# Two key buffers at the start, and four 16-node additions per round behind a transpose, in a graph layer on one core

## The chip, the cores and the metric

The kernel runs on one core of a Trainium2 chip. The metric is the device time of one execution in microseconds (us). Before the change it is 2062.51 us, the median of three runs (2060.89 to 2064.04).

## The reference

A graph layer over 12,500 nodes of 128 features and 400,000 edges, sorted by destination:

```python
Xs = X[src]
m_data = Xs @ W_data.T + b_data
m_ctrl = Xs @ W_control.T + b_control
msg = jnp.where((edge_types == 0)[:, None], m_data, m_ctrl)
agg = jax.ops.segment_sum(msg, dst, num_segments=X.shape[0])
out = jax.nn.relu(agg + (X @ W_self.T + b_self))
y = layernorm(x + out)          # over the 128 features, eps 1e-5
```

## The kernel before

The kernel never forms messages. It sums source rows by destination and edge type first, and multiplies the two sums of a node by the two weight matrices afterwards. Nodes are split into two sets.

**Dense nodes** (the first 6400). Their sums are products of x with a matrix of edge counts. TensorE builds the counts of 20 nodes (a batch) out of one-hot matrices that VectorE makes (`make_onehots`, L1176 to L1190). ScalarE, and for the last half batch of eight VectorE (`move_last`, L1195 to L1204), copies them out of PSUM, and TensorE multiplies them with x (`apply`, L738). There are 640 batches, one in each **step** s of the main loop, eight to a pass. In step s TensorE does `apply(s-8)`, then `build(s)` (L719), then whatever small job that step has. At the start of a pass `apply` waits for `move_last`. The one-hots need keys of the edges. Fifteen chunks of keys are prepared on VectorE (`prepare_dense_keys`, L1079 to L1090), chunk 1 in step 1 and chunks 2 to 14 in steps 9 to 21, and stored to memory by SyncE's queue (`store_dkeys`, L499 to L505). All chunks share one buffer, `dk_f`, which lies over `x_u`, so chunk c waits until the store of chunk c-1 has landed. Later the keys are gathered back in groups of 240 nodes. To find a group's place, a window of 129 destinations is loaded (`load_window`, L482), and `find_starts` (L1118 to L1129) reads it. `win_i` is a single buffer.

**Sparse nodes** (the rest) go through 154 **rounds**. In a round GpSimd gathers ten times 128 rows of x (L637, two rounds ahead at most), TensorE multiplies them with one-hots (`gather_sums`, L699), in step s-1. ScalarE copies the result to `sg`: 128 partitions, each one place of a (half, sub-window, type, node) list, by 128 features. In step s TensorE turns it into `misc` (`turn_sums`, L746 and L747), and VectorE adds it to the accumulator `acc` at a place read from memory (`add_sums`, L1234 to L1249). Each of a round's two groups covers two windows of 16 nodes that overlap (the second begins 9 nodes on). The matrix `turn_picks` of ones and zeros adds the overlap in the matmul, so `misc` holds 32 nodes of two types per group.

Every small job of TensorE writes the one bank `misc`: rounds, key groups, and for each of 114 output units a transpose of x (`turn_x`, L763) and the products (L778 to L789). Before each job TensorE waits on `misc_free` for the reader of the job before it. For a round that is VectorE's increment at L1249, after both groups are added. Rounds sit in steps 4 and 0 of a pass of eight; the planner at the top of the kernel puts every other job into the next free step. TensorE works strictly in the written order, as do the others.

Of the kernel before, what the change touches and what calls it, by code (L numbers as in the profile page):

```python
# [13 lines left out]
ALU = mybir.AluOpType  # L14
# [3 lines left out]
P = 128  # L18
D = 128
GT = 5  # L20
WIN = 32
HALF_WIN = 16
LATE_WIN = 9
# [30 lines left out]
DKCH = 15  # L54
# [5 lines left out]
def gnn_resnorm(nc, x, src, dst, etype, w_data, b_data, w_ctrl, b_ctrl, w_self, b_self, out):  # L60
# [6 lines left out]
    KGROUPS = -(-DENSE // KNODES)  # L67
# [48 lines left out]
    for e in range(EPOCHS):  # L116
        base = WIN_0 + EPOCH_NODES * e
        n0 = max(base, DENSE)
        n1 = N if e == EPOCHS - 1 else base + EPOCH_NODES
        k = -(-(n1 - n0) // P)  # L120
# [23 lines left out]
    for v in units:  # L144
        if not v.dense:
            e = (v.n0 - WIN_0) // EPOCH_NODES
# [59 lines left out]
    with ctx:  # L206
        def sb(name, shape, dt=F32):
            return ctx.enter_context(nc.sbuf_tensor(name, shape, dt))
# [5 lines left out]
        def sem(name):  # L214
            return ctx.enter_context(nc.semaphore(name))
# [16 lines left out]
        acc = sb("acc", [P, 2, 2, SPAN])  # L232
# [7 lines left out]
        ident = sb("ident", [P, P])  # L240
# [5 lines left out]
        part_f = sb("part_f", [P, 10])  # L246
# [3 lines left out]
        low = sb("low", [P, 2])  # L250
        base_p = sb("base_p", [P, 3, 2])
        sg = sb("sg", [P, 129])
        turn_picks = sb("turn_picks", [P, P])
        fin = sb("fin", [P, 2, COLS])
        fin_deg = sb("fin_deg", [P, DEG_RING * KNODES], BF16)
        deg_c = sb("deg_c", [P, 2, 9], BF16)
# [1 line left out]
        deg_new = sb("deg_new", [P, 2])  # L258
        deg_ok = sb("deg_ok", [P, 2])
        x_u = sb("x_u", [P, 3, D])  # L260
        x_t = sb("x_t", [P, 2, P])
        y_sb = sb("y_sb", [P, 2, D])
        stats = sb("stats", [P, 2, 6])
        mv = sb("mv", [P, 2, 2])
        std = sb("std", [P, 2])
# [6 lines left out]
        ptr = sb("ptr", [P, 4, 2])  # L272
# [34 lines left out]
        iota_q, iota_p = iotas[:, 0:2 * XBLOCKS], iotas[:, 2 * XBLOCKS:2 * XBLOCKS + P]  # L307
# [20 lines left out]
        K = KCOLS  # L328
# [1 line left out]
        acc_1 = acc_1f.bitcast(I32)  # L330
        dk_in = [[acc_1[:, K * (3 * i + k):K * (3 * i + k + 1)] for k in range(3)] for i in range(2)]
        dk_p = acc_1[:, 6 * K:7 * K]
        dk_f = x_u[:, :, :].rearrange("p u d -> p (u d)")[:, 0:3 * K]
        b9_f = acc_1f[0:9, 7 * K:7 * K + D]
        b9_h = acc_1f[0:9, 7 * K + D:7 * K + D + D // 2].bitcast(BF16)
        assert 7 * K + D + D // 2 <= 2 * SPAN and 3 * K <= 3 * D

        acc_all = cnt_raw[:, 0:XBLOCKS * P]
        late_x = x_u[:, 0, :]
        late_xt = x_t[:, 0, :]  # L340
        LW = 256
        iota_w = acc[:, 0, 0, 0:LW]
# [12 lines left out]
        misc = psum("misc")  # L355
# [32 lines left out]
        weights_turned = sem("weights_turned")  # L388
        wt_ready = sem("wt_ready")
        dkeys_ready = sem("dkeys_ready")  # L390
        dkeys_written = sem("dkeys_written")
        tail_ready = sem("tail_ready")
        hi_ready = sem("hi_ready")
        x2_ready = sem("x2_ready")
        win_taken = sem("win_taken")
# [9 lines left out]
        acc_step = sem("acc_step")  # L405
# [6 lines left out]
        misc_full = sem("misc_full")  # L412
# [40 lines left out]
        key_flat = key_dram.rearrange("r w -> (r w)").rearrange("(c p e) -> c p e", c=DKCH, p=P)  # L453
        key0_flat = key0_dram.rearrange("r w -> (r w)").rearrange("(p e) -> p e", p=P)
        key1_flat = key1_dram.rearrange("r w -> (r w)").rearrange("(c p e) -> c p e", c=2, p=P)
# [8 lines left out]
            return KEY_TILES * P if g >= 3 else K * P * min(2, g + 1)  # L464

        def key_stores(c):
            return 16 * (c + 1 + min(c + 1, 2) + 1)

        KEY_STORES = key_stores(DKCH - 1)

        def late_rows(u):
            return min(P, N - u * P)
# [3 lines left out]
        def _(sp):  # L476
# [22 lines left out]
            def store_dkeys(c):  # L499
                sp.wait_ge(dkeys_ready, c + 1)  # L500
                if c == 0:
                    sp.dma_start(key0_flat, dk_f).then_inc(dkeys_written, 16)
                if c < 2:
                    sp.dma_start(key1_flat[c, :, :], dk_f).then_inc(dkeys_written, 16)
                sp.dma_start(key_flat[c, :, :], dk_f).then_inc(dkeys_written, 16)  # L505

            def load_x(c):
                full = XB if c < XCH - 1 else XB - 1
# [25 lines left out]
            for k, b in enumerate((b_data, b_ctrl, b_self)):  # L534
                sp.dma_start(bias3[k:k + 1, :], b.rearrange("(o d) -> o d", o=1)).then_inc(bias3_loaded, 16)
                sp.dma_start(b9_f[3 * k:3 * k + 3, :], b.partition_broadcast(3)).then_inc(bias9_loaded, 16)
            for c in range(1, DKCH):
                store_dkeys(c)
                if c + 2 < DKCH:
                    load_dkeys(c + 2)  # L540
            sp.wait_ge(dkeys_written, KEY_STORES)
            for i in range(3):
                load_unit(i, units[i].n0, units[i].r)
            for s in range(STEPS):
                g = ptr_at(s + 2)
                if g is not None and g + 1 < KGROUPS:
                    sp.wait_ge(win_taken, g + 1)
                    load_window(g + 1)
                if s - 3 in out_at:
                    i = out_at[s - 3]  # L550
                    if i + 3 < UNITS:
                        sp.wait_ge(y_ready, i + 1)
                        load_unit(i + 3, units[i + 3].n0, units[i + 3].r)
                    store_unit(i, units[i].n0, units[i].r)
                if s == TURN_END - 24:
                    sp.wait_ge(ptr_ready, KGROUPS)
                    sp.wait_ge(keys_ready, KGROUPS)
                    for j, v in enumerate(ends):
                        sp.dma_start(end_x[0:v.r, j, :], x[v.n0:v.n0 + v.r, :]).then_inc(end_loaded, 16)
# [14 lines left out]
            with sp.If(general > 0):  # L574
# [9 lines left out]
                for u in range(LATE_UNITS):  # L584
                    i = UNITS + u
# [11 lines left out]
        def _(pool):  # L597
# [18 lines left out]
            def gather_keys(g):  # L616

                pool.wait_ge(ptr_ready, g + 1)
                if g in (0, 1, 3):
                    pool.wait_ge(dkeys_written, key_stores(0 if g == 0 else 1 if g == 1 else DKCH - 1))  # L620
                pool.indirect_dma_start(
                    out=key_raw[:, :], out_offset=None, in_=keys_in(g),
                    in_offset=bass.IndirectOffsetOnAxis(ap=key_at[:, 0:1], axis=1),
                ).then_inc(keys_gathered, 16)
# [35 lines left out]
        def _(pe):  # L660
# [82 lines left out]
            def turn_sums(ps):  # L743

                pe.wait_ge(sg_ready, ps + 1)
                pe.matmul(misc[0:66, P:P + 64], zg_picks[:, :], picks, start=True, stop=True)  # L746
                pe.matmul(misc[:, 0:P], sg[:, 0:D], turn_picks[:, :], start=True, stop=True).then_inc(misc_full, 1)  # L747

            def turn_keys(g):

# [92 lines left out]
            with pe.If(general > 0):  # L843
# [11 lines left out]
                for u in range(LATE_UNITS):  # L855
                    i = UNITS + u
# [140 lines left out]
        def _(dve):  # L997
            steps = [0]

            def step(ins):  # L1000

                ins.then_inc(dve_step, 1)
                steps[0] += 1
                dve.wait_ge(dve_step, steps[0])
# [74 lines left out]
            def prepare_dense_keys(c):  # L1079

                s_i, d_i, t_i = dk_in[c % 2]
                kf = dk_f.rearrange("p (e k) -> p e k", k=3)
                dve.wait_ge(dkeys_loaded[c % 2], 48 * (c // 2 + 1))
                if c:
                    dve.wait_ge(dkeys_written, key_stores(c - 1))
                dve.tensor_copy(kf[:, :, 2], d_i)
                step(dve.tensor_single_scalar(dk_p, s_i, P - 1, ALU.bitwise_and))
                dve.tensor_copy(kf[:, :, 0], dk_p)
                step(dve.tensor_single_scalar(s_i, s_i, 7, ALU.logical_shift_right))
                dve.scalar_tensor_tensor(out=kf[:, :, 1], in0=t_i, scalar=float(XBLOCKS), in1=s_i,  # L1090
                                         op0=ALU.mult, op1=ALU.add).then_inc(dkeys_ready, 1)
# [5 lines left out]
            for k in range(3):  # L1097
# [3 lines left out]
            step(dve.tensor_tensor(part_f[:, 0:1], ptr[:, 0, 0:1], ptr[:, 1, 0:1], ALU.add))  # L1101
            step(dve.tensor_single_scalar(part_f[:, 1:2], part_f[:, 0:1], 1.0, ALU.add))
            nodes = part_f[:, 0:2]
            node_w, pair_w, turn_w = ptr[:, 1, 0:1], ptr[:, 1, 1:2], ptr[:, 2, 0:1]
            step(dve.scalar_tensor_tensor(out=node_w, in0=part_f[:, 7:8], scalar=float(LATE_WIN),
                                          in1=part_f[:, 8:9], op0=ALU.mult, op1=ALU.add))
            step(dve.scalar_tensor_tensor(out=pair_w, in0=part_f[:, 6:7], scalar=float(WIN),
                                          in1=node_w, op0=ALU.mult, op1=ALU.add))
            dve.tensor_scalar(picks, iota_p[:, 0:64], pair_w, None, ALU.is_equal)
            step(dve.scalar_tensor_tensor(out=turn_w, in0=part_f[:, 6:7], scalar=float(WIN),  # L1110
                                          in1=pair_w, op0=ALU.mult, op1=ALU.add))
            step(dve.scalar_tensor_tensor(out=turn_w, in0=part_f[:, 9:10], scalar=float(WIN),
                                          in1=turn_w, op0=ALU.mult, op1=ALU.add))
            dve.tensor_scalar(turn_picks[:, :], iota_p, turn_w, None, ALU.is_equal)
            dve.tensor_copy(t_mask[:, 1:2], part_f[:, 9:10])
            dve.tensor_scalar(t_mask[:, 0:1], part_f[:, 9:10], -1.0, 1.0, ALU.mult, ALU.add)

# [116 lines left out]
            def add_sums(ps):  # L1234

                e = ps // EPOCH
                bases = [dve.value_load(off_i[:, 2 * ps + g:2 * ps + g + 1], min_val=0, max_val=SPAN - WIN)
                         for g in range(2)]
                dve.wait_ge(misc_full, job[sum_step[ps]] + 1)
                for g, base in enumerate(bases):  # L1240
                    if ps or g:
                        dve.wait_ge(acc_step, 2 * ps + g)
                    dw = acc_deg[0:2, e % 2, bass.ds(base, WIN)]
                    dve.tensor_tensor(dw, misc[0:2, P + 32 * g:P + 32 * g + 32], dw, ALU.add)  # L1244
                    aw = acc[:, e % 2, :, bass.ds(base, WIN)]
                    dve.tensor_tensor(aw, misc[:, 64 * g:64 * g + 64].rearrange("p (t w) -> p t w", t=2), aw,  # L1246
                                      ALU.add).then_inc(acc_step, 1)
                dve.wait_ge(acc_step, 2 * ps + 2)
                dve.sem_inc(misc_free, 1)  # L1249

            def next_epoch(e):
# [181 lines left out]
```

## Time and profile before

| | |
|---|---|
| median of 3 runs | 2062.51 us |
| the profiled execution: its time, its span | 2064.31 us, 2062.5 us |
| TensorE matmuls busy | 95% |
| weight loads, VectorE, ScalarE, GpSimd busy | 84%, 72%, 64%, 72% |

The profile is of one execution. A busy share counts instructions in flight, and matmuls overlap, so 95% doesn't say that nothing is left; it says where to look for what sets the order. Where rows show start times, differences of starts are used rather than durations.

### The profile page before, as it was taken

The page shows a single profiled execution, that of the slowest core. Times are in us where ns is not written, and L with a number is a line of the kernel's source. Part 1 is how long each engine was busy: PE and PEld are TensorE (multiplying, and loading weights), DVE is VectorE, ACT ScalarE, POOL GpSimd, SP SyncE. Part 2 cuts the span into 40 slices and gives each one's busy share as a digit, 9 for nine tenths or more (in the row PEclk, how much of TensorE's full clock was granted, in tenths as well). Part 3 has the DMA queues.
Part 4 walks back from the last instruction along what each step waited for, and adds up shares of the span by engine and source line. Part 5 has one row for each costly group of instructions (what it writes and reads, how often), then busy time and mean ns, then how long its engine had stood idle before and what let it go on. Part 6 is the DMA issues. An engine that isn't in the chain of part 4 may idle for free.

```text
span 2062.5 us, 62886 instructions
## 1 busy us (share of the span) xinstructions
PE 1960.9 (95%) x25383; PEld 1725.1 (84%) x25383; DVE 1476.4 (72%) x3669; ACT 1320.5 (64%) x1940; POOL 1491.6 (72%) x1581
## 2 busy tenths in 40 slices
PE   4879999999999999999999999999999999999997
PEld 2668888888888888888888888888888888888887
DVE  8867777777677777777766776777676777677773
ACT  5546666666666666666666666666666666666663
POOL 6767776777677776777777777677776777777771
PEclk9989999999999999999999999999999999999999
DMA  9332222222222222222222222222222222222221
GB/s 240 98 85 65 61 67 54 67 61 66 54 66 61 66 62 60 62 66 61 65 58 68 60 69 61 58 63 66 59 69 56 64 64 65 61 61 65 65 61 27
DMA packets 109893, 139.47 MB, mean 68 GB/s; under 512 B 39083, under 2 KB 82739, under 8 KB 109599
## 3 DMA queue, kind: packets, MB, share of 16 engines
q0 software_dynamic: 51008, 106.33, 19.9%
q1 hardware_dynamic: 58591, 29.04, 5.3%
q8 instruction: 205, 3.36, 0.7%
q14 instruction: 89, 0.73, 0.1%
HBM read 125.87 MB, written 9.39 MB: 66 GB/s over the span
## 4 chain that ended last, share of the span: by engine, by line
PE 83%; DVE 8%; issue 3%; DMA 2%; ACT 2%; POOL 2%; DVEq 1%; SPq 0%; ACTq 0%; POOLq 0%
PE apply_ps L738 53%; PE build L719 15%; PE sum_ps L699 4%; PE misc L747 2%; DVE cnt L1204 2%; POOL rows L637 1%; ACT cnt L906 1%; PE misc L763 1%; PE misc L788 1%; PE misc L780 1%; PE misc L778 1%; PE misc L786 1%; DVE hot_q L1190 1%; PE misc L746 1%; DVE hot_p L1187 1%
## 5 line engine op out<-in xcount | busy, mean ns | idle before, releaser
L637 POOL DMA_INDIRECT rows<-in_x,src_t x1540 | 1463.1, 950 | 519.1 <-issue 466.3
L906 ACT ACTIVATE cnt<-build 128x1000 fp32r<-128x1000 f32 (+1 forms) x1200 | 1125.0, 986 | 676.2 <-PE build L719 602.5
L738 PE MATMUL apply_ps<-cnt,x 128*128 128x320 f32 x7840 | 1320.2, 317 | 43.9 <-DVE cnt L1204 27.3
L738 PEld LDWEIGHTS apply_ps<-cnt,x 128*128 128x128 f32 x7840 | 1167.4, 190 | 79.4 <-issue 30.7
L1187 DVE TENSOR_TENSOR hot_p<-const_ps,key_pq 128x1280 bf16<-128x1280 bf16 x640 | 525.7, 821 | 369.6 <-PE build L719 367.3
L719 PEld LDWEIGHTS build<-hot_q,hot_p 64*128 64x128 bf16 x12800 | 307.0, 94 | 138.8 <-issue 124.3
L1190 DVE TENSOR_TENSOR hot_q<-const_ps,key_pq 128x1000 bf16<-128x1000 bf16 (+1 forms) x640 | 421.2, 658 | 0.0
L719 PE MATMUL build<-hot_q,hot_p 64*128 64x100 bf16 (+1 forms) x12800 | 403.9, 205 | 12.0 <-DVE hot_q L1190 7.0
L699 PE MATMUL sum_ps<-rows,hot 128*32 128x129 f32 x3080 | 139.8, 282 | 5.2 <-DMA rows<-in_x,src_t 5.0
L1204 DVE CAST cnt<-build 128x1000 fp32r<-128x1000 f32 x80 | 94.1, 1176 | 50.1 <-PE build L719 46.3
L699 PEld LDWEIGHTS sum_ps<-rows,hot 128*32 128x32 f32 x3080 | 92.3, 110 | 23.1 <-DMA rows<-in_x,src_t 10.2
L1244 DVE TENSOR_TENSOR acc_deg<-misc,acc_deg 2x32 f32 x308 | 55.2, 179 | 36.9 <-issue 4.9
L1073 DVE TENSOR_TENSOR hot<-const_ps,key_t 128x320 f32<-128x320 bf16 x154 | 72.9, 473 | 1.3 <-PE sum_ps L699 1.3
L747 PE MATMUL misc<-turn_picks,sg 128*128 128x128 f32 x308 | 73.5, 321 | 0.0
L1246 DVE TENSOR_TENSOR acc<-misc,acc 128x64 f32 x308 | 69.3, 225 | 0.3 <-issue 0.3
L931 ACT ACTIVATE y_sb<-y_sb,shift,rstd 107x128 f32<-107x128 f32 (+4 forms) x114 | 56.3, 494 | 5.0 <-DVE shift L1275 5.0
L892 ACT ACTIVATE sg<-sum_ps 128x129 f32<-128x129 f32 x154 | 43.7, 284 | 14.1 <-PE sum_ps L699 14.1
L1262 DVE SCALAR_TENSOR_TENSOR y_sb<-misc,x_u 107x128 f32<-107x128 f32 (+4 forms) x114 | 32.2, 283 | 24.9 <-DMA out<-y_sb 14.6
L894 ACT ACTIVATE zg_picks<-t_mask,sg 128x2 f16<-128x2 f32 x154 | 45.6, 296 | 5.0
L747 PEld LDWEIGHTS misc<-turn_picks,sg 128*128 128x128 f32 x308 | 47.5, 195 | 0.0
L1268 DVE BATCH_NORM_STATS2 stats<-y_sb 107x6 f32<-107x128 f32 (+4 forms) x114 | 33.0, 289 | 14.8 <-DVE y_sb L1262 13.9
L763 PE MATMUL misc<-ident,x_u 107*128 107x107 f32 (+4 forms) x114 | 34.9, 306 | 7.1 <-DVEq L1286 6.1
(192 smaller groups left out, 887.2 us busy)
## 6 DMA issues: line engine op xcount, KB each, us to landing
rows<-in_x,src_t POOLq DMA_INDIRECT x1540
x_raw<-in_x SPq DMA_DIRECT2D x13, 448.0 KB, 8.2
key_dram<-x_u SPq DMA_DIRECT2D x18, 162.0 KB
x_u<-in_x SPq DMA_DIRECT2D x39, 64.0 KB
out<-y_sb SPq DMA_DIRECT2D x39, 64.0 KB
x_u<-in_x SPq DMA_DIRECT2D x36, 53.5 KB
out<-y_sb SPq DMA_DIRECT2D x36, 53.5 KB
win_i<-in_dst SPq DMA_DIRECT2D x27, 64.0 KB
```

The source lines that it names most:

```text
L637: pool.indirect_dma_start(out=rows[:, slot, 0:D], out_offset=None, in_=x, in_offset=bass.IndirectOffsetOnAxis(ap=src_t[:, col:col + 1], ax ...
L699: last = pe.matmul(sum_ps[o:o + WIN, 0:D + 1], hot[:, g * GT + j, :], rows[:, slot, 0:D + 1], start=(j in (0, EARLY_TILES)), stop=(j in (E ...
L719: last = pe.matmul(build_ps[z][:, o:o + 2 * H], hot_p[part, s + pair, :, r], hot_q[part, s + pair, 0:2 * H, r], start=True, stop=True)
L738: last = pe.matmul(sums, x2[:, b, D * k:D * k + D], counts(b - half * HALVES[0], half), start=(b == 0 and k == 0), stop=(r == TURNS - 1 an ...
L747: pe.matmul(misc[:, 0:P], sg[:, 0:D], turn_picks[:, :], start=True, stop=True).then_inc(misc_full, 1)
L906: act.activation(o, i.rearrange("p h (m b) -> p b h m", b=H), ACT.Copy).then_inc(evacuated, 1)
L931: act.activation(y_sb[0:r, i % 2, :], y_sb[0:r, i % 2, :], ACT.Identity, bias=shift[0:r, i % 2:i % 2 + 1], scale=rstd[0:r, i % 2:i % 2 + 1 ...
L1073: dve.tensor_tensor(hot[:, :, :].rearrange("p (g j) c -> p g j c", g=2), hot_table.rearrange("p (j c) -> p j c", c=WIN).unsqueeze(1) .to_b ...
L1187: dve.tensor_tensor(hot_p[:, s:s + QUADS, :, :], table_p.unsqueeze(1).to_broadcast([P, QUADS, P, 2]), keys_p.unsqueeze(2).to_broadcast([P, ...
L1190: dve.tensor_tensor(hot_q[:, s:s + QUADS, 0:2 * H, :], table_q[half].unsqueeze(1).to_broadcast([P, QUADS, 2 * H, 2]), keys_q.unsqueeze(2). ...
L1204: dve.tensor_copy(o, i.rearrange("p h (m b) -> p b h m", b=H)).then_inc(last_moved, 1)
L1246: dve.tensor_tensor(aw, misc[:, 64 * g:64 * g + 64].rearrange("p (t w) -> p t w", t=2), aw, ALU.add).then_inc(acc_step, 1)
```

## The change

Four edits that belong together in two pairs. (1) The dense keys get a second buffer: `xt_y` replaces `x_t` and `y_sb`, whose memory the second buffer uses before any unit does. Chunk c then waits for the store of chunk c-2, and stores are counted on two semaphores. (2) SyncE loads window 2 before the stores of chunks 1 to 14 instead of after them. (3) `turn_picks` is gone: `sg` is turned by a transpose with the identity. (4) `misc` then holds four pieces of 16 nodes by two types, and VectorE adds each on its own, with a wait for the piece before.

```diff
-        dk_f = x_u[:, :, :].rearrange("p u d -> p (u d)")[:, 0:3 * K]
+        dk_f = [x_u[:, :, :].rearrange("p u d -> p (u d)")[:, 0:3 * K], xt_y[:, 0:3 * K]]
...
+            sp.wait_ge(win_taken, 2)
+            load_window(2)
             for c in range(1, DKCH):
                 store_dkeys(c)
                 if c + 2 < DKCH:
                     load_dkeys(c + 2)
-            sp.wait_ge(dkeys_written, KEY_STORES)
+            for c in (DKCH - 2, DKCH - 1):
+                sp.wait_ge(dkeys_written[c % 2], key_stores(c))
             for i in range(3):
                 load_unit(i, units[i].n0, units[i].r)
             for s in range(STEPS):
                 g = ptr_at(s + 2)
-                if g is not None and g + 1 < KGROUPS:
+                if g is not None and 3 <= g + 1 < KGROUPS:
...
-                pe.matmul(misc[:, 0:P], sg[:, 0:D], turn_picks[:, :], start=True, stop=True).then_inc(misc_full, 1)
+                pe.transpose(misc[:, 0:P], sg[:, 0:D], ident[:, :]).then_inc(misc_full, 1)
...
-                if c:
-                    dve.wait_ge(dkeys_written, key_stores(c - 1))
+                if c >= 2:
+                    dve.wait_ge(dkeys_written[c % 2], key_stores(c - 2))
...
                     if ps or g:
-                        dve.wait_ge(acc_step, 2 * ps + g)
+                        dve.wait_ge(acc_step, 4 * ps + 2 * g)
                     dw = acc_deg[0:2, e % 2, bass.ds(base, WIN)]
                     dve.tensor_tensor(dw, misc[0:2, P + 32 * g:P + 32 * g + 32], dw, ALU.add)
-                    aw = acc[:, e % 2, :, bass.ds(base, WIN)]
-                    dve.tensor_tensor(aw, misc[:, 64 * g:64 * g + 64].rearrange("p (t w) -> p t w", t=2), aw,
-                                      ALU.add).then_inc(acc_step, 1)
-                dve.wait_ge(acc_step, 2 * ps + 2)
+                    for h in range(2):
+                        if h:
+                            dve.wait_ge(acc_step, 4 * ps + 2 * g + 1)
+                        aw = acc[:, e % 2, :, bass.ds(base, WIN)][:, :, LATE_WIN * h:LATE_WIN * h + HALF_WIN]
+                        o = 64 * g + WIN * h
+                        dve.tensor_tensor(aw, misc[:, o:o + WIN].rearrange("p (t w) -> p t w", t=2), aw,
+                                          ALU.add).then_inc(acc_step, 1)
+                dve.wait_ge(acc_step, 4 * ps + 4)
                 dve.sem_inc(misc_free, 1)
```

## Rows read from the trace of the kernel before

**Rows 1.** The page: busy time of the engines, and TensorE's granted clock in 40 slices.
```profile
PE 1960.9 (95%) x25383; PEld 1725.1 (84%) x25383; DVE 1476.4 (72%) x3669; ACT 1320.5 (64%) x1940; POOL 1491.6 (72%) x1581
...
PEclk9989999999999999999999999999999999999999
```
**Rows 2.** The page: the chain that ended last, by engine.
```profile
PE 83%; DVE 8%; issue 3%; DMA 2%; ACT 2%; POOL 2%; DVEq 1%; SPq 0%; ACTq 0%; POOLq 0%
```
**Rows 3.** TensorE in order of time, 121 to 134 us: start, duration, what.
```profile
121.11 0.85 PE L699 MATMUL sum_ps<-rows,hot 128*32 128x129 f32 x20
132.38 3.54 PE L738 MATMUL apply_ps<-cnt,x 128*128 128x320 f32 x12 [10.42 <-DVE cnt L1204]
```
**Rows 4.** VectorE in order of time, 122 to 132 us.
```profile
122.17 0.47 DVE L1086 CAST x_u<-acc 128x108 f32<-128x108 int32 x1 [1.68 <-DMA key_dram<-x_u]
...
129.54 0.15 DVE L1124 TENSOR_SCALAR win_f<-part_i 128x1 f32<-128x1 int32 x1 [4.89 <-DMA win_i<-in_dst]
...
131.09 1.19 DVE L1204 CAST cnt<-build 128x1000 fp32r<-128x1000 f32 x1
```
**Rows 5.** SyncE's queue in order of time, 119 to 127 us.
```profile
119.23 4.51 SPq L505 DMA_DIRECT2D key_dram<-x_u  x2
...
126.83 0.38 SPq L484 DMA_DIRECT2D win_i<-in_dst  x1
```
**Rows 6.** Waits between 100 and 170 us: total, times, longest.
```profile
DVE x_u L1086 <- DMA key_dram<-x_u: 6.4, 5, 2.8
DVE win_f L1124 <- DMA win_i<-in_dst: 4.9, 1, 4.9
```
**Rows 7.** Windows: length, busy time and instructions by engine, granted clock, DMA share, GB/s.
```profile
130.00:140.00 10.00, 7.62 (x69) 6.90 (x69) 6.06 (x15) 2.05 (x3) 5.76 (x7) 0.63 0.22 53
```
**Rows 8.** TensorE around a round and its next job, 1010 to 1015 us.
```profile
1010.88 0.63 PE L719 MATMUL build<-hot_q,hot_p 64*128 64x100 bf16 x20
...
1011.72 2.01 PE L738 MATMUL apply_ps<-cnt,x 128*128 128x320 f32 x12
...
1013.66 0.63 PE L719 MATMUL build<-hot_q,hot_p 64*128 64x100 bf16 x20
...
1014.21 0.14 PEld L763 LDWEIGHTS misc<-ident,x_u 107*128 107x128 f32 x1
```
**Rows 9.** TensorE over a step without a small job, 1050 to 1053 us.
```profile
1050.14 0.63 PE L719 MATMUL build<-hot_q,hot_p 64*128 64x100 bf16 x20
...
1052.70 0.49 PE L719 MATMUL build<-hot_q,hot_p 64*128 64x100 bf16 x14
```
**Rows 10.** The chain of waits between 139 and 143 us: start, length, what.
```profile
139.91 0.26 PE misc L763
...
142.47 0.42 PE misc L677 x2
```
**Rows 11.** VectorE's additions of the same round, 1013 us.
```profile
1013.15 0.23 DVE L1246 TENSOR_TENSOR acc<-misc,acc 128x64 f32 x1
...
1013.51 0.18 DVE L1244 TENSOR_TENSOR acc_deg<-misc,acc_deg 2x32 f32 x1
...
1013.64 0.23 DVE L1246 TENSOR_TENSOR acc<-misc,acc 128x64 f32 x1
```
**Rows 12.** A later round: its last addition, and a job that waited for it.
```profile
1026.14 0.23 DVE L1246 TENSOR_TENSOR acc<-misc,acc 128x64 f32 x1
...
1026.48 0.14 PEld L763 LDWEIGHTS misc<-ident,x_u 128*128 128x128 f32 x1 [0.20 <-DVEq L1249]
```
**Rows 13.** GpSimd's gathers over the run, and its wait for TensorE.
```profile
L637 POOL DMA_INDIRECT rows<-in_x,src_t x1540 | 1463.1, 950 | 519.1 <-issue 466.3
...
POOL rows L637 <- PE sum_ps L699: 45.4, 9, 8.9
```
**Rows 14.** The last gather of round 16, and the sums that use it.
```profile
247.65 0.94 POOL L637 DMA_INDIRECT rows<-in_x,src_t  x1 [0.30 <-issue]
...
254.87 0.85 PE L699 MATMUL sum_ps<-rows,hot 128*32 128x129 f32 x20
```

More of the change, by code:

```diff
@@ L252, in gnn_resnorm @@
         sg = sb("sg", [P, 129])
-        turn_picks = sb("turn_picks", [P, P])
         fin = sb("fin", [P, 2, COLS])
@@ L260, in gnn_resnorm @@
         x_u = sb("x_u", [P, 3, D])
-        x_t = sb("x_t", [P, 2, P])
-        y_sb = sb("y_sb", [P, 2, D])
+        xt_y = sb("xt_y", [P, 2 * P + 2 * D])
         stats = sb("stats", [P, 2, 6])
@@ L339, in gnn_resnorm @@
         late_x = x_u[:, 0, :]
+        x_t = xt_y[:, 0:2 * P].rearrange("p (i r) -> p i r", r=P)
+        y_sb = xt_y[:, 2 * P:2 * P + 2 * D].rearrange("p (i d) -> p i d", d=D)
         late_xt = x_t[:, 0, :]
@@ L390, in gnn_resnorm @@
         dkeys_ready = sem("dkeys_ready")
-        dkeys_written = sem("dkeys_written")
+        dkeys_written = [sem(f"dkeys_written{i}") for i in range(2)]
         tail_ready = sem("tail_ready")
@@ L466, in key_stores @@
         def key_stores(c):
-            return 16 * (c + 1 + min(c + 1, 2) + 1)
-        KEY_STORES = key_stores(DKCH - 1)
+            return 16 * (c // 2 + (3 if c % 2 == 0 else 2))
         def late_rows(u):
@@ L501, in store_dkeys @@
                 if c == 0:
-                    sp.dma_start(key0_flat, dk_f).then_inc(dkeys_written, 16)
+                    sp.dma_start(key0_flat, dk_f[0]).then_inc(dkeys_written[0], 16)
                 if c < 2:
-                    sp.dma_start(key1_flat[c, :, :], dk_f).then_inc(dkeys_written, 16)
-                sp.dma_start(key_flat[c, :, :], dk_f).then_inc(dkeys_written, 16)
+                    sp.dma_start(key1_flat[c, :, :], dk_f[c]).then_inc(dkeys_written[c], 16)
+                sp.dma_start(key_flat[c, :, :], dk_f[c % 2]).then_inc(dkeys_written[c % 2], 16)
             def load_x(c):
@@ L618, in gather_keys @@
                 pool.wait_ge(ptr_ready, g + 1)
-                if g in (0, 1, 3):
-                    pool.wait_ge(dkeys_written, key_stores(0 if g == 0 else 1 if g == 1 else DKCH - 1))
+                for c in {0: (0,), 1: (0, 1), 3: (DKCH - 2, DKCH - 1)}.get(g, ()):
+                    pool.wait_ge(dkeys_written[c % 2], key_stores(c))
                 pool.indirect_dma_start(
@@ L1081, in prepare_dense_keys @@
                 s_i, d_i, t_i = dk_in[c % 2]
-                kf = dk_f.rearrange("p (e k) -> p e k", k=3)
+                kf = dk_f[c % 2].rearrange("p (e k) -> p e k", k=3)
                 dve.wait_ge(dkeys_loaded[c % 2], 48 * (c // 2 + 1))
-                if c:
-                    dve.wait_ge(dkeys_written, key_stores(c - 1))
+                if c >= 2:
+                    dve.wait_ge(dkeys_written[c % 2], key_stores(c - 2))
                 dve.tensor_copy(kf[:, :, 2], d_i)
@@ L1103, in _ @@
             nodes = part_f[:, 0:2]
-            node_w, pair_w, turn_w = ptr[:, 1, 0:1], ptr[:, 1, 1:2], ptr[:, 2, 0:1]
+            node_w, pair_w = ptr[:, 1, 0:1], ptr[:, 1, 1:2]
             step(dve.scalar_tensor_tensor(out=node_w, in0=part_f[:, 7:8], scalar=float(LATE_WIN),
@@ L1109, in _ @@
             dve.tensor_scalar(picks, iota_p[:, 0:64], pair_w, None, ALU.is_equal)
[L1110 to L1114, printed above, removed]
             dve.tensor_copy(t_mask[:, 1:2], part_f[:, 9:10])
```

## The prediction

> **What bounds the kernel now.** I read the page first: TensorE is in flight 95% of the time at a granted clock of 9 tenths or more everywhere but in one slice [rows 1], and the chain that ended last runs 83% over it and 8% over VectorE [rows 2]. So time is what TensorE's ordered list costs, plus the places where it stands still. Next I looked for those places, in the first slices. The largest is at 122 us: the sums of a round begin at 121.11 and take 0.85, and the next `apply` starts at 132.38, after 10.42 us of idling that VectorE's copy L1204 ended [rows 3]. VectorE's own order says why the copy was late. It waited 1.68 us for a key store, and then 4.89 us for window 2 [rows 4]. SyncE's queue shows that window 2 was not slow but late: the last two stores lie between 119.23 and 123.74, then the queue waited for them to land, and the window went out at 126.83 [rows 5]. The copy (131.09, 1.19 long) followed. Between 100 and 170 us VectorE lost 6.4 us to stores and 4.9 us to that window [rows 6]. Behind the hole the clock was down (0.63 over 130 to 140 us [rows 7]): twelve matmuls took 3.54 us [rows 3], and 2.01 us at full clock [rows 8].
>
> Last I read one round step by step, since it repeats 154 times.
>
> **Change part by part, a: the hole.** With window 2 on its way before the stores, and chunk c waiting only for the store of chunk c-2, both waits should go. What remains of the pass boundary: VectorE makes its window matrices and copies `fin` (129.54 to 131.09, 1.6 us), and the copy takes 1.19 us. TensorE has 0.85 us of sums to do meanwhile, so I leave it 2.2 us of idling out of 10.42: 8.2 gained. In the steps just before, VectorE's store waits (6.4 us) also held TensorE up; it has its own pace there, and I count 3 us for that (half of 6.4, the rest is VectorE's slack). The clock: with a stand of about 2 us, like the ordinary pass boundaries, that show no fall in the slices [rows 1], the 1.5 us on twelve matmuls come back, and about 0.7 on the builds and the round behind them (the same ratio on some 1.6 us of work). Sum 13.4 us. Bounds: 8, if loads of the next keys (three issues behind each store on the same queue) replace the store waits and the clock falls all the same; 14.5, if VectorE never holds TensorE there. The stores now start only after window 1 was taken, in step 2, long before step 9 asks for chunk 2: nothing. Unit loads leave the queue earlier: nothing, the first unit is turned in step 25. `xt_y` has no users before that either.
>
> **b: the transpose.** A two-pass product of this size holds the chain 0.42 us (L677), a transpose 0.26 (L763) [rows 10]: 0.16 less. From another side: a step with a round lasts 2.78 us from build to build [rows 8], one with no job 2.56 [rows 9], so all three matmuls of `turn_sums` cost 0.22, and 0.16 of that is the most a transpose could save; half of it, one of two equal passes, 0.11, is the least. I take 0.15.
>
> **c: the additions.** From the start of the first L1246 (1013.15) to the end of the last (1013.64 + 0.23) is 0.72 us. An addition followed by a wait on itself has its successor 0.36 later, 0.23 of work and 0.14 behind its end; the pair without a wait is 0.13 apart [rows 11]. No row shows a piece of 128x32. The nearest has as many elements in a partition: 2x32, 0.18 us [rows 11]. So a piece and its wait are 0.32, and the new stretch is 0.32 + 0.32 + 0.13 + 0.32 + 0.18 = 1.27, or 0.55 more; with the 0.01 that rounding hides, 0.56. Bounds: 0.75, where a piece takes 0.23 like the whole; 0.17, where the wait inside a group adds nothing and pieces follow in 0.13.
>
> The Trainium skill speaks for that lower end. Its page "VectorE: DVE Perf Modes", section "The DRAIN you can't avoid", says that a semaphore behind each of eight copies costs nothing over one behind the last. This trace doesn't agree for small additions (0.36 with the wait, 0.13 without [rows 11]). By the rule a round would grow by 0.17 us, the first rival below.
>
> **What c costs TensorE** decides the sign. VectorE has the time itself (72% busy). But the bank `misc` is freed behind the last addition, and TensorE's next job waits for that with everything behind it. The planner's arithmetic gives for the 154 rounds: 68 with no job in the next step (the next is three steps off or more, so nothing is paid), 63 followed at once by a unit's transpose, and 23 by a unit's products. In such a pair VectorE starts adding after its one-hots, which are tied to the build of the round's step, not to `turn_sums`; so an earlier `turn_sums` gives nothing there, and each delay beyond the slack is TensorE's. The slack: in the round shown the last addition ends at 1013.87 and the next job's weight load starts at 1014.21, a gap of 0.34 [rows 8, 11]. The least gap, where TensorE did wait, is 0.11 (1026.37 to 1026.48) [rows 12]. Of the 86, 10 are at 0.11, and the other 76 have 0.34 in the mean. So 76 x (0.56 + 0.11 - 0.34) = 25.1, and 10 x 0.56 = 5.6: 30.7 us lost. In the other 68 the transpose pays: 68 x 0.15 = 10.2 us gained.
>
> **Sum.** 30.7 - 10.2 - 13.4 = +7.1 us on the profiled execution's 2064.3 us: 2071.4. That execution lies 1.8 over the median of 2062.5, so 2069.6, about 2070. Slower by 0.35%. It breaks even where 76 x (d - 0.23) + 10 x d = 23.6, at a growth d of 0.48 us per round.
>
> **Rivals.**
> - *The added waits are nearly free* (d 0.17). Then 76 x (0.17 - 0.23) + 10 x 0.17 = -2.9, and with 10.2 and 13.4 it is 26 us faster. GpSimd takes something off: its gathers repeat every 0.95 + 0.30 = 1.25 us, 1925 us in all, with 45.4 us of waiting for TensorE in the whole run [rows 13]. 2040. Against it: the 0.36 beside 0.13. For it: no row has a wait between two L1246. This is the case on the other side, and it needs d under 0.48. Chance 0.12.
> - *The hole doesn't close.* VectorE then waits for key loads in place of stores, since four issues per chunk stay in one queue, and the change buys 5 us (the window's wait alone): 2078. For it: one SyncE queue carries both. Against: loads are two chunks ahead. Chance 0.12.
> - *VectorE's longer rounds reach TensorE elsewhere.* 26 key groups are prepared in a step that also has a round; if each of those passes the 0.56 on to a build, 26 x 0.56 = 15 us more: 2084. Half of it, 2077, is as likely. Against: a share of 72%. Chance 0.13.
> - *The gathers can't follow.* With TensorE 13 us earlier, round 16 has less than its 6.3 us between last gather (248.59) and sums (254.87) [rows 14]; GpSimd itself gets earlier only by what it waited at the hole (8.9 us, the longest in [rows 13]). That leaves 6.3 - (13.4 - 8.9) = 1.8 us for the landing. It would give back 1 or 2 us around 250 us, and more only if TensorE's rounds get faster: 2072. Chance 0.08.
>
> **Numbers.** The forecast has 0.55 and its own range 2062 to 2078 (d from 0.47 to 0.64). The 8-in-10 range is 2050 to 2086: above, d of 0.75 (76 x 0.52 + 7.5 = 47.0 lost, less 23.6) gives 2086; below it reaches half way to the first rival. A measurement of this kernel tells 0.2%, or 4 us, from no change. Slower by more: most of the forecast (0.31 of 0.55) and nearly all of the second, third and fourth rivals, 0.59. Within: 0.19. Faster: 0.22, the first rival and the low end of the forecast.
>
> **What would show it.** a right: no wait for `win_i` at L1124, TensorE idle 2 to 3 us near 120 us in place of 10.42, a clock of 1.00 over 120 to 140. b right: L747 once per round, about 0.26 in the chain, a round's step near 2.63. c right: 616 records of the addition at about 0.18, 0.32 apart, and a gap of 0.11 before the next job in nearly all 86 pairs, with VectorE's semaphore named as releaser some 80 times. GpSimd's wait for TensorE grows past 45.4. The forecast is wrong if pieces are under 0.25 apart, if those 86 jobs don't wait, or if TensorE still stands over 5 us near 120.

## The result, and the profile after

The kernel after takes 2088.60 us (median of 4 runs, 2088.41 to 2088.73), against 2063.28 us for the kernel before in the same runs: a ratio of 1.0123, 95% interval 1.0105 to 1.0140. It is slower by 25.3 us, where 7 were forecast and 2086 was the end of the range. The mechanism that decided is the forecast's; what it costs was forecast too low, and a part of it was not in the sum at all.

The page of the kernel after, busy time and chain:

```profile
PE 1943.4 (93%) x25229; PEld 1701.6 (82%) x25229; DVE 1522.9 (73%) x3974; ACT 1321.2 (63%) x1940; POOL 1495.4 (72%) x1581
...
PE 69%; DVE 16%; issue 6%; DVEq 4%; ACT 2%; POOL 2%; DMA 1%; SPq 1%; ACTq 0%; POOLq 0%
```

Against [rows 1, 2] TensorE is in flight 17.5 us less, so the transpose did what it was for; VectorE's share of the chain doubled. It has 46.5 us more work; whether that load or the waits are the cause is tried below (y4, x5). The long waits of the kernel after show where the chain crosses over (total, times, longest):

```profile
PEld misc L764 <- DVEq L1249: 43.0, 63, 1.5
...
PEld build L720 <- DVE hot_q L1186: 20.8, 49, 5.6
...
PEld misc L787 <- DVEq L1249: 8.8, 15, 0.6
...
PEld misc L779 <- DVEq L1249: 5.1, 8, 0.8
```

L1249 is VectorE's increment of `misc_free` behind a round. TensorE's next job, a unit's transpose (L764) or its products (L779, L787), waited for it 86 times, 56.9 us: the 86 pairs of the prediction, all of them, and in each the weight load starts 0.11 us behind the end of the last addition. One pair in order of time, on both engines:

```profile
1019.60 0.63 PE L720 MATMUL build<-hot_q,hot_p 64*128 64x100 bf16 x20
...
1020.67 0.14 PEld L764 LDWEIGHTS misc<-ident,x_u 107*128 107x128 f32 x1 [0.60 <-DVEq L1249]
```

The chain through the same stretch says what TensorE was waiting for (start, length, what):

```profile
1017.63 0.33 DVE hot_p L1183
...
1018.29 0.30 DVEq L1233
...
1018.59 0.23 DVE hot_q L1186
...
1019.23 0.20 DVE acc L1246
...
1019.57 0.20 DVE acc L1246
...
1020.03 0.20 DVE acc L1246
...
1020.37 0.20 DVE acc L1246
...
1020.67 0.31 PE misc L764
```

From the first addition to the end of the last, before the semaphore, it is 1019.23 to 1020.57 in these rows, 0.60 us longer (unrounded) than the 0.72 of [rows 11], where 0.56 more was forecast. In the mean of all 154 rounds it is 0.61 longer. A piece takes 0.19, and the piece that waits for it starts 0.34 later. The rows by form:

```profile
L1246 DVE TENSOR_TENSOR acc<-misc,acc 128x32 f32 x616 | 118.2, 192 | 45.9 <-issue 1.1 <-DVE acc L1246 0.8
...
L748 PE MATMUL misc<-ident,sg 128*128 128x128 f32 x154 | 47.6, 309 | 0.0
```

At the start, TensorE in order of time:

```profile
90.55 0.98 PE L720 MATMUL build<-hot_q,hot_p 64*128 64x96 bf16 x20 [5.34 <-DVE hot_q L1186]
...
118.34 0.85 PE L700 MATMUL sum_ps<-rows,hot 128*32 128x129 f32 x20
123.02 3.37 PE L739 MATMUL apply_ps<-cnt,x 128*128 128x320 f32 x12 [3.83 <-DVE cnt L1200]
```

The stand of TensorE, 10.42 us before [rows 3], is 3.83. No wait for `win_i` is left. But twelve matmuls behind it still take 3.37 us.

**Step by step.** The main loop has the same steps in both kernels. I took the start of the last weight load of each step's build in both traces and, from step 32 on, summed by how much each step grew, by the small job that lies in it:

| job in the step | steps | mean, us | sum, us |
|---|---|---|---|
| a round (`turn_sums`) | 145 | -0.158 | -22.9 |
| a unit's transpose, right behind a round | 62 | +0.595 | +36.9 |
| a unit's products, right behind a round | 23 | +0.511 | +11.8 |
| key group | 25 | +0.138 | +3.5 |
| all others | 353 | +0.014 | +4.8 |

At step 31 the kernel after was 9.5 us ahead. The forecast had 13.4. In a pair two rows of the table go together: the round's own step gets 0.158 us shorter, and the step behind it grows.

### The profile page after: what moved, and what is told of

Its sections match the earlier page's. It is cut to its first block, busy times and chain, and to the rows that moved or that the text cites. A ratio compares the mean times of both kernels' runs of the same rounds, so it can differ in the third digit from the quotient of the medians.

```text
span 2086.6 us, 63191 instructions
## 1 busy us (share of the span) xinstructions
PE 1943.4 (93%) x25229; PEld 1701.6 (82%) x25229; DVE 1522.9 (73%) x3974; ACT 1321.2 (63%) x1940; POOL 1495.4 (72%) x1581
## 4 chain that ended last, share of the span: by engine, by line
PE 69%; DVE 16%; issue 6%; DVEq 4%; ACT 2%; POOL 2%; DMA 1%; SPq 1%; ACTq 0%; POOLq 0%
PE apply_ps L739 45%; PE build L720 13%; PE sum_ps L700 4%; DVE acc L1246 4%; DVE hot_p L1183 3%; DVEq L1233 2%; DVE hot_q L1186 2%; DVE cnt L1200 2%; POOL rows L638 1%; PE misc L764 1%; ACT cnt L907 1%; PE misc L781 1%; PE misc L789 1%; PE misc L779 1%; PE misc L787 1%
## 5 line engine op out<-in xcount | busy, mean ns | idle before, releaser
L1246 DVE TENSOR_TENSOR acc<-misc,acc 128x32 f32 x616 | 118.2, 192 | 45.9 <-issue 1.1
L764 PE MATMUL misc<-ident,x_u 107*128 107x107 f32 (+4 forms) x114 | 35.4, 310 | 41.3 <-DVEq L1249 33.6
L764 PEld LDWEIGHTS misc<-ident,x_u 107*128 107x128 f32 (+4 forms) x114 | 15.8, 139 | 56.2 <-DVEq L1249 43.0
L932 ACT ACTIVATE xt_y<-xt_y,shift,rstd 107x128 f32<-107x128 f32 (+4 forms) x114 | 56.3, 494 | 7.2 <-DVE shift L1275 7.2
L1262 DVE SCALAR_TENSOR_TENSOR xt_y<-misc,x_u 107x128 f32<-107x128 f32 (+4 forms) x114 | 32.2, 282 | 25.2 <-DMA out<-xt_y 15.4
L748 PE MATMUL misc<-ident,sg 128*128 128x128 f32 x154 | 47.6, 309 | 0.0
L1268 DVE BATCH_NORM_STATS2 stats<-xt_y 107x6 f32<-107x128 f32 (+4 forms) x114 | 32.9, 289 | 15.3 <-DVE xt_y L1262 15.0
```

The costliest lines, as they stand in the source:

```text
L764: pe.transpose(misc[:, 0:v.r], x_u[0:v.r, i % 3, :], ident[0:v.r, 0:v.r]).then_inc(misc_full, 1)
L932: act.activation(y_sb[0:r, i % 2, :], y_sb[0:r, i % 2, :], ACT.Identity, bias=shift[0:r, i % 2:i % 2 + 1], scale=rstd[0:r, i % 2:i % 2 + 1 ...
L1246: dve.tensor_tensor(aw, misc[:, o:o + WIN].rearrange("p (t w) -> p t w", t=2), aw, ALU.add).then_inc(acc_step, 1)
```

## The experiments

Each run is compared with the kernel before on the same chip; what is said against the kernel after uses its 2088.6.

| run | us | before | ratio (95%) |
|---|---|---|---|
| y1_keys | 2050.66 | 2064.21 | 0.9936 (0.9919 to 0.9952) |
| y3_matmul | 2095.63 | 2064.21 | 1.0153 (1.0136 to 1.0170) |
| y4_apart | 2045.03 | 2064.21 | 0.9913 (0.9897 to 0.9930) |
| y5_space_before | 2048.60 | 2064.21 | 0.9923 (0.9906 to 0.9939) |
| x5_space | 2038.47 | 2063.74 | 0.9876 (0.9860 to 0.9893) |
| x6_first | 2065.38 | 2063.74 | 1.0009 (0.9998 to 1.0019) |
| x7_window | 2059.70 | 2063.74 | 0.9980 (0.9970 to 0.9990) |
| x8_late_window | 2093.14 | 2063.74 | 1.0144 (1.0127 to 1.0161) |
| z1_keys_space | 2034.59 | 2064.76 | 0.9852 (0.9836 to 0.9869) |
| z2_space_apart | 2037.51 | 2064.76 | 0.9866 (0.9850 to 0.9883) |

**Is it the wait, or VectorE's load? (y4_apart)** The pieces of a group no longer overlap, so the second needs no wait. The instructions stay; which nodes the sums land on changes.

```diff
-                        if h:
-                            dve.wait_ge(acc_step, 4 * ps + 2 * g + 1)
-                        aw = acc[:, e % 2, :, bass.ds(base, WIN)][:, :, LATE_WIN * h:LATE_WIN * h + HALF_WIN]
+                        aw = acc[:, e % 2, :, bass.ds(base, WIN)][:, :, HALF_WIN * h:HALF_WIN * h + HALF_WIN]
```

> The kernel after with a group's second piece added 16 nodes on, not 9, and so without the wait for the first; the sums land on other nodes. Instructions and VectorE's busy time are the same. Theory: the bank is free 0.2 us later than before and not 0.6, and the pairs cost nearly nothing: 2045 to 2052. Rival (VectorE's 46 us more of busy time are the cause): 2085 to 2089.

43.6 us off the kernel after, in the theory's range. VectorE's additions of one round:

```profile
1007.99 0.32 DVE L1244 TENSOR_TENSOR acc<-misc,acc 128x32 f32 x2
...
1008.58 0.32 DVE L1244 TENSOR_TENSOR acc<-misc,acc 128x32 f32 x2
```

Two pieces take 0.32 together, and the stretch is 0.91: 0.19 over before, so 0.41 less than after. In the step table the pairs' steps fell by 0.40 (62 transposes) and 0.41 (23 products). TensorE gets back one for one what the bank is held less. The expectation was wrong in one point: VectorE's busy time did not stay. Pieces that overlap in time count once, and so it fell by 20.4 of the 46.5 us:

```profile
PE 1939.4 (95%) x25229; PEld 1698.3 (83%) x25229; DVE 1502.5 (74%) x3974; ACT 1320.5 (65%) x1940; POOL 1491.6 (73%) x1581
```

The other 26.1 us are still there, in a kernel that is faster than the one before. So what counts is how long the additions hold the bank. That the busy time as such is not the main cause x5 below shows better: there VectorE is busy for 1520.8 us, within 2.1 of the kernel after.

**Does the cheaper product pay in a pair? (y3_matmul)**

```diff
-                pe.transpose(misc[:, 0:P], sg[:, 0:D], ident[:, :])
+                pe.matmul(misc[:, 0:P], sg[:, 0:D], ident[:, :], start=True, stop=True)
```

> The kernel after with a two-pass product by the identity in place of the transpose; same values. Theory: in 86 pairs the next job waits for VectorE anyway, so the dearer product costs only in the other 68 rounds: 11 us over the kernel after, 2099. Rival (each of 154 rounds pays 0.16 us): 25 us, 2113.

7.0 us over the kernel after, where the theory had 11 and the rival 25. The step table tells it: 145 rounds +0.164 each, and the steps behind them in pairs -0.163 and -0.164. In a pair nothing is gained by turning faster, the wait takes it; only the other rounds pay (60 x 0.164 = 9.8 from step 32 on, some of it made good elsewhere).

**No job behind a round (x5_space).** The planner keeps the step behind each round free.

```diff
     def place(s):
-        while s in taken:
+        while s in taken or s - 1 in after_sums:
             s += 1
...
+    after_sums.update(sum_step)
```

> The kernel after with a planner that puts no job into the step behind a round. VectorE's instructions are the same. Theory: the bank is free by then, the 48.6 us of the pairs go: 2038 to 2045. Rival (VectorE's own load holds the builds up): 2083 to 2090.

2038.47, in the theory's range: 50.1 us below the kernel after, and below the kernel before. Not all of it is the pairs: the same planner gives 15.6 us with the rounds of before (y5 below).

**Additions ahead of the one-hots (x6_first).**

```diff
+                if sums_at(s) is not None:
+                    add_sums(sums_at(s))
                 if batch_at(s + 2) is not None:
                     make_onehots(s + 2)
...
-                if sums_at(s) is not None:
-                    add_sums(sums_at(s))
```

> The kernel after with VectorE's additions ahead of its one-hots in a round's step. Theory: the additions begin when the turned sums are there, about 1 us sooner after the build, so the bank is free before the next job: 2038 to 2045, as with the other planner. Rival (one-hots come late and TensorE's builds wait for them): over 2060.

2065.38: 23.2 us off the kernel after, but in the rival's range (over 2060). The pairs' steps fell by 0.51 and 0.49, 42.7 us in all, so the wait did go; but other steps grew, keys by 5.0, lone transposes by 6.0, and the start (step 31) by 3.6. Its waits:

```profile
PEld build L720 <- DVE hot_q L1186: 30.2, 55, 4.7
...
PEld misc L764 <- DVEq L1286: 12.7, 6, 2.2
...
PEld misc L764 <- DVEq L1249: 7.2, 13, 1.7
```

VectorE's lateness went from the bank to the one-hots, as the rival said (20.8 us of waits in the kernel after, 30.2 here), and to the unit outputs (L1286).

**The keys alone (y1_keys), the window alone (x7_window), the window late (x8_late_window).** In y1 the two buffers and the early window stand, the rounds are those of before. x7 has one buffer and the early window, x8 the whole change with these lines undone:

```diff
-            sp.wait_ge(win_taken, 2)
-            load_window(2)
             for c in range(1, DKCH):
...
-                if g is not None and 3 <= g + 1 < KGROUPS:
+                if g is not None and g + 1 < KGROUPS:
```

> The two key buffers and the early window alone, again, on another chip. The early window alone gave 5.6 us by step 31. Theory: both give 9 to 11 us: 2052 to 2055. Rival (the forecast's 13.4): 2049 to 2050.

> The kernel before with the early window alone, one key buffer. Theory: VectorE's 4.9 us wait for the window goes, its waits for stores stay: 5 us less, 2058. Rival (the hole is VectorE's lateness from the stores, and the window's wait only took its place): under 2 us less, 2061 to 2063.

> The kernel after with window 2 behind the stores again, two key buffers. Theory: the queue sends the window only after the last store has landed, near 121 us, and VectorE waits for it until about 124: 3 to 5 us over the kernel after, 2092 to 2094. Rival (two buffers alone close the hole): 2088 to 2090.

The first `apply` behind the stand in y1:

```profile
120.22 2.95 PE L740 MATMUL apply_ps<-cnt,x 128*128 128x320 f32 x12 [2.36 <-DVE cnt L1206]
```

The same in x7:

```profile
126.27 3.54 PE L740 MATMUL apply_ps<-cnt,x 128*128 128x320 f32 x12 [6.28 <-DVE cnt L1206]
```

The same in x8, and VectorE's wait before it:

```profile
125.80 2.47 PE L737 MATMUL apply_ps<-cnt,x 128*128 128x320 f32 x8 [8.53 <-DVE cnt L1198]
```
```profile
122.96 0.15 DVE L1118 TENSOR_SCALAR win_f<-part_i 128x1 f32<-128x1 int32 x1 [5.01 <-DMA win_i<-in_dst]
```

y1 gave 13.5 us: nearer to the rival of its expectation, which was my own forecast, than to the theory, and the stand is 2.36 where 2.2 was forecast. x7 gave 4.0 us (6.28 of the stand left). x8 is 4.5 us over the kernel after (3.1 by step 31): with the window behind the stores the 5.01 us wait is back, two buffers or not. So each edit takes its own part of the hole: the window some 4 us, the second buffer the rest. The buffer without the window was tried only with the new rounds (x8).

**The planner with the kernel before (y5_space_before), with keys and old rounds (z1_keys_space), with short additions (z2_space_apart).** All have the planner of x5.

> The kernel before with the planner that puts no job behind a round. Theory: before, the 86 pairs waited hardly at all (10 of them), so the planner alone gives 0 to 4 us: 2059 to 2064. Rival (the planner is good by itself, whatever the rounds cost): below 2050.

> Key buffers, early window and the planner with nothing behind a round, with the rounds of the kernel before. By sums of the runs so far: 2063 less 13.5 (keys) less 15 (planner) is 2034 to 2036. If the transpose is worth its 24 us once nothing waits for the additions, the same planner with the new rounds (2038.5) should have been 2011; that it was not says VectorE's longer rounds eat it. Theory: 2034 to 2037, the old rounds are as good or better. Rival (the two gains overlap and the new rounds are worth having): 2043 or more.

> The kernel after with the planner and with disjoint pieces that need no wait in a group; the sums land on other nodes. If VectorE's 0.4 us per round still reaches TensorE's builds with the planner: 2025 to 2031. If the gathers set the pace by then (1.25 us each): 2035 to 2039, no gain over the planner with the change's own pieces.

y5 missed: 15.6 us, where 0 to 4 were expected. Its steps don't line up with those of before, so the waits have to say it. At the pass boundary `apply` waits for ScalarE's last copy; before and then y5:

```profile
PEld apply_ps L738 <- ACT cnt L906: 30.5, 31, 1.5
```
```profile
PEld apply_ps L739 <- ACT cnt L907: 12.9, 14, 1.4
```

Jobs moved out of the step behind a round lie in other steps, and in about half of those boundaries this wait is gone. That a moved job fills it was read from the waits, not tried. z1 is the fastest version run: 2034.59, ratio 0.9852, 54 us below the kernel after, with the old rounds; x5, with the new ones, is 3.9 us above it, but the two intervals overlap, so the new rounds are worth nothing there; that they do harm isn't shown. z2 is no faster. What x5, z1 and z2 have in common is the gathers. The chain that ended last in z1, where GpSimd had 2% before [rows 2]:

```profile
POOL 53%; PE 25%; issue 18%; DMA 1%; DVE 1%; SPq 1%; ACT 0%; DVEq 0%; POOLq 0%; ACTq 0%
```

It is 51% in x5 and 57% in z2. Sums waiting for rows, and GpSimd waiting for TensorE, in z1 and in z2:

```profile
PEld sum_ps L702 <- DMA rows<-in_x,src_t: 18.1, 20, 2.0
...
POOL rows L640 <- PE sum_ps L702: 17.0, 7, 4.8
```
```profile
PEld sum_ps L701 <- DMA rows<-in_x,src_t: 38.2, 42, 2.5
...
POOL rows L639 <- PE sum_ps L701: 18.2, 8, 6.5
```

GpSimd waited 45.4 us in all before [rows 13], and 17 and 18 here; TensorE waits for rows 42 times in z2.

**Four runs that say nothing of the cause.** x1_keys, x2_sums, x3_matmul and x4_apart ran on a chip where the kernel before took 3653.8 us. They took 3649.4, 3645.4, 3650.2 and 3643.0 (ratios 0.9991, 0.9976, 0.9989, 0.9977; each interval about 0.001 either way). TensorE's mean granted clock was 0.78 there, but that is not the whole reason: TensorE was in flight for only 69% of x1's span, and in `apply` it stood still 532 times with nothing to wait for that the trace shows ("issue"; 2 times and 3.4 us in the kernel before):

```profile
PE apply_ps L740 <- issue: 440.6, 532, 2.1
```

What made it stand is open. Three of the four were repeated as y1, y3, y4. x2, the transpose and pieces alone, was not.

> The two key buffers and the early window alone; rounds as before. Theory: their gain is what step 31 of the two profiles shows, 9.3 us, or up to 2 us more because the rounds before it are short again: 2052 to 2054. Rival (the forecast's term of 13.4 us was right and the longer rounds hid part of it): 2049 to 2050.

> The transpose and the four pieces alone; keys as before. Theory: TensorE pays 0.57 us in each of 85 jobs right behind a round (48.6 us) and gets 0.16 us back in each round (24): with some 8 us elsewhere 2095 to 2099. Rival (parts work on each other at the start): outside that by over 3 us.

> The kernel after with a two-pass product by the identity in place of the transpose; values the same. Theory: in the 86 pairs the next job waits for VectorE anyway, so the dearer product costs only in the other 68 rounds, 68 x 0.16 = 11 us over the kernel after: 2099. Rival (each of the 154 rounds pays its 0.16 us): 25 us, 2113.

> The kernel after with the second piece of a group added 16 nodes on, not 9, so that it needs no wait for the first; the sums land on other nodes. As many VectorE instructions and as much busy time. Theory: pieces are 0.13 us apart, a round frees the bank 0.2 us later than before and not 0.6, and the pairs cost nearly nothing: 2045 to 2052. Rival (VectorE's busy time of 46 us more is the cause): 2085 to 2089.

One thing can be read from x2: there the new rounds with the old keys were 8.4 us faster than the kernel before, while with the new keys, on other chips, they cost some 38 us (2088.6 against y1's 2050.7). One reading is that VectorE is less often late where TensorE takes that much longer; that was not tried.

## Why the prediction was wrong

- **Direction and mechanism: right.** TensorE's next job waits for the bank in exactly the 86 pairs; y4 and y3 show it from both sides.
- **The step that failed: what the longer rounds cost outside the pairs was put at nothing.** I had said of c that "VectorE has the time itself (72% busy)", and the sum has no term for it. The forecast's cost of the rounds is 30.7 - 10.2 = 20.5 us. The traces of the kernel after and of y1, which has the old rounds and is otherwise the same, are 37.7 us apart at the last build: 35.3 in the pairs (net of the transpose), -9.5 in the other rounds, and 11.8 that the forecast didn't have. Of these, 3.4 lie before step 32 (with one pair among them, some 0.4), and 8.4 in later steps that have neither a round nor the second half of a pair. y4, with additions 0.41 us shorter per round, gets back 4.7 us by step 31, and then 2.8 in the key steps and 2.9 in the others. So it is the length of VectorE's additions that reaches TensorE there too. One way is through the one-hots. The builds' wait for them, before, in y1 and in y4, where the kernel after has 20.8:

```profile
PEld build L719 <- DVE hot_q L1190: 12.4, 19, 3.3
```
```profile
PEld build L721 <- DVE hot_q L1192: 8.2, 16, 3.1
```
```profile
PEld build L720 <- DVE hot_q L1186: 11.9, 30, 3.1
```

The largest single one is at the start. VectorE has key chunks to prepare in each of the steps 9 to 21, and in step 12 a key group and the biases besides, and the build of step 15 waited 5.34 us for it (3.08 in the kernel before, 2.83 in y1). The chain that leads to this build runs over VectorE from 76 us on, and the four additions of the round of step 12 are in it, from 81.70 to 82.92 us.

- **The pairs' price: too low, the smaller part.** The forecast's growth of 0.56 us is 0.60. With it the forecast's own sum, 76 x (0.60 + 0.11 - 0.34) + 10 x 0.60, is 34.1, and the table gives 85 x 0.572 - 85 x 0.158 = 35.2 net, against 30.7.
- **The transpose: right.** 0.158 us per round for 0.15. Only in rounds without a job behind: 60 x 0.158 = 9.5 from step 32 on, for 10.2. (For 12 of the 68 the next job is two steps off, not three or more as I wrote; 10 of them lie behind step 32, and one of these grew, by 0.11 us.)
- **The hole: right by itself.** Alone it is worth 13.5 us (y1, 12.9 of it by step 31), and 13.4 was added. Together with the longer rounds the kernel after was only 9.5 us ahead at step 31. That the new rounds cost 3.4 us there, on top of the new keys, is measured; whether they would with the old keys isn't, since the rounds alone ran only as x2.
- **The third rival was a term, not an alternative.** Against the kernel before, key steps and others grew by 3.5 + 4.8 = 8.3 us. The forecast gave it a chance of 0.13, at 15 us or half of it, and put zero in the sum.
- **The clock: wrong, with little effect.** It was to be 1.00 over 120 to 140 us, and was 0.83 over the first half of that. After a stand of 3.83 us, and of 2.36 in y1, twelve matmuls took 3.37 and 2.95 us, not 2.01. The steps before the stand gave more than the 3 us I had put (y1 was 4.1 us ahead by step 23), so y1 still came to 13.5.
- **The first rival: ruled out.** A piece that waits starts 0.34 us behind the one before, one that doesn't 0.13 (y4: two in 0.32). So the semaphore rule of the Trainium skill's page "VectorE: DVE Perf Modes", section "The DRAIN you can't avoid", which carried this rival, doesn't hold for these additions of 0.19 us.
- **The gathers** set no limit in the kernel after (GpSimd waits 63.1 us in all), but they do with the planner of x5 (over half of the chain in x5, z1 and z2).

Forecast against measured: pairs 30.7 and 35.2; other rounds -10.2 and -9.5; keys, window and start -13.4 and -9.5; elsewhere 0 and 8.3; sum 7.1 and 24.5. The two profiled executions, from which these are taken, are 24.1 us apart (2088.41 and 2064.31); the medians are 25.3 apart. One slip in the forecast's ranges: a growth of 0.64 gives 2076.5 on the median, and the 2078 written for it is on the profiled execution.

## What to carry to other kernels

Where engines share one bank or buffer through a semaphore, price an edit by how long the holder keeps it, and look for who stands right behind. Cheaper work in front of such a wait bought nothing here (y3). A busy share of 72% did not mean that longer work costs nothing: list the steps in which that engine has more to do than the step gives it. Moving the waiter (one condition in the planner) was worth more than any change of the work, 50 us (15.6 in the kernel before), and then neither the new rounds nor shorter additions made it faster, since another engine set the pace. The start was 12.9 us ahead with one pair of edits and 9.5 with both: run each edit alone and then together before adding up terms from the same stretch of time.

## What the runs showed of the hardware that was not expected

TensorE's granted clock doesn't follow from the length of the stand alone. After 2.36 us in y1 twelve matmuls took 2.95 us; after 2.65 us in y4, at the same place, they took 2.00, as at full clock (2.01 [rows 8]). The row of y4:

```profile
120.30 2.00 PE L739 MATMUL apply_ps<-cnt,x 128*128 128x320 f32 x12 [2.65 <-DVE cnt L1200]
```

The window from 120 to 130 us of y1 and then of y4, with the granted clock as the third number from the end:

```profile
120.00:130.00 10.00, 9.78 (x104) 8.79 (x105) 5.68 (x13) 4.41 (x6) 7.56 (x8) 0.83 0.29 77
```
```profile
120.00:130.00 10.00, 9.29 (x110) 8.44 (x111) 7.09 (x18) 5.47 (x7) 7.56 (x9) 1.00 0.30 78
```

A mean of 0.83 means that part of the window was at the lower level, 1.2 GHz, and the rest at 2.4. In the 10 us before, TensorE was busy for 7.87 us in y1 and for 7.65 in y4, so that doesn't tell the two apart. What does is open.
